# Expert weights in single blocks of 512 KB: a ring of three blocks in place of three pairs

## The chip, the cores and the metric

One core of a Trainium2 chip runs the whole program. The metric is the device time of one execution in microseconds, from runs of the same kernel on the same chip. A profile of one execution stands beside it; its times count from the start of its span.

## What is computed

Sixteen sequences x[b] of 512 rows and 512 features go through two layers.

```python
# layer 0, conditioned on one number t per sequence
h = noise_encoding(t, 128); h = silu(h @ W1 + b1); h = h @ W2 + b2
scale, shift = h @ Wsc + bsc, h @ Wsh + bsh
out = silu(scale * layernorm(x) + shift) @ W_in + b_in      # norm over rows and features
out = silu(scale * layernorm(out) + shift) @ W_out + b_out
x = out + x
# layer 1: one of 8 experts per sequence, 512 -> 2048 -> 512
g = gelu(x @ Wi[e] + bi[e]);  r = g @ Wo[e] + bo[e] + x
y = layernorm_row(r) * gamma[e] + beta[e]                    # norm over features
```

## The kernel before

Everything is kept transposed, features on the 128 partitions. A float32 product is made of three products of rounded parts: each operand is split into `hi` (rounded to float32r, a copy on ScalarE) and `lo` (the rest, a subtraction on VectorE), and `three` (L550) issues hi*hi, hi*lo and lo*hi.

**The loop.** The hidden width of 2048 is cut in 16 blocks of 128 (`HT`), so there are 256 steps `k`, 16 for each sequence. A tick `k` of the main loop (L699 for TensorE, L844 for ScalarE, L1199 for VectorE) issues `up(k)`, the first expert product of block k into a bank of `hid_ps` (12 matmuls), and `down(k-2)`, the second product of block k-2 into the four banks of `out_acc` (12 matmuls). Layer 0 of the next sequence is spread over the same ticks by the table `STAGE_AT` (L73): in ticks 2 to 5 one tile each of W_IN, in 11 to 14 one tile each of W_OUT (12 matmuls each). Below, the tick is counted within a sequence, 0 to 15. For the norm of x: `stats` in tick 13 (X_STATS, -3), `mv_out` (X_OUT) and `mv_back` (X_BACK) in tick 14, which send the statistics to DRAM and back to every partition, `totals` and `centre` in tick 15, `affine` and `silu` in tick 0, the split into `h_hi` and `h_lo` in tick 1, the first W_IN tile in tick 2. For the inner norm, `mv_back` is in tick 6 and `totals` in tick 7. The second sequence has its own table `STAGE_AT_1`.

**The splits of the weights.** In tick k ScalarE issues `gelu(k-1)`, `wi_hi_part(k+1)` (L744) and `wo_hi_part(k)` (L752); VectorE issues the lo part of gelu, `wi_lo_part(k+1)` and `wo_lo_part(k)` (L1048), which counts up the semaphore `s_wolo`. These are the readers of the weights' landing place `stage`. In the last ticks (`LAST` is 6) the downs are put off to the end, so that four ups follow each other.

**The queue.** All large loads and stores are issued by SyncE (SP), in order: a wait in its program holds up everything behind it. `expert_w` in DRAM holds the blocks in pairs, two blocks of 512 KB (half of it Wi, half Wo) side by side. `load_pair(p)` (L403) fetches a pair of 1024 KB into slot p % 3 of `stage`; the three slots take 24 KB of each partition. Pairs 0 to 2 wait for the head to be done with the slot, later ones for `s_wolo` of pair p-3. Between the pairs SP issues the other transfers: `load_x(b+2)` behind the fifth pair of a sequence, `store_y(b-2)` and `load_rows(b-1)` (gamma and beta, broadcast) behind its first pair, `load_bi(b+1)` at its end. The ACT queue carries only the small transfers of the statistics.

**The head.** Before the loop, the conditioning network runs from weights that are parked in places used later for other things: W2 in slot 0 of `stage`, the four parts of the conditioning weights `cond_raw(m)` in slots 1 and 2 (L242 to L245), a row of ones in `rows`. `s_mm2` counts that the W2 products are done, `s_mmcond` counts the four conditioning products. `w_raw[1]`, the place of W_out, is `x2_turned`, which later holds the transposed sequence.

Of the kernel before, what the change touches and what calls it, by code (L numbers as in the profile page):

```python
# [33 lines left out]
P = 128  # L34
# [7 lines left out]
B, S, D = 16, 512, 512  # L42
EMB = 128
EXPERTS, HID = 8, 2048
# [110 lines left out]
def build(nc, xT, itok, head, W1, W2, cond_w, bias_rows, affine0, affine, W_in, W_out,  # L155
          expert_w, expert_bi, expert_rows, mv_dram, y):
    ctx = ExitStack()
    with ctx:
        def sb(name, shape, dt=F32):
            return ctx.enter_context(nc.sbuf_tensor(name, shape, dt))  # L160
# [15 lines left out]
        x2_hi = [sb(f"x2_hi{n}", [P, DC, S], F32R) for n in range(2)]  # L176
        x2_lo = [sb(f"x2_lo{n}", [P, DC, S], F32R) for n in range(2)]
        NSTAGE = 3
        stage = sb("stage", [P, NSTAGE, 2, 2, 512])
        NWI, NWO = 2, 3  # L180
        wi_hi = sb("wi_hi", [P, NWI, DC, P], F32R)
        wi_lo = sb("wi_lo", [P, NWI, DC, P], F32R)
# [56 lines left out]
        w1_raw = g_sb[:, 0, :]  # L239
        t_sb, cc, small_sb = head_sb[:, 0:B], head_sb[:, B:B + 3], head_sb[:, B + 3:]  # L240
        b_in = small_sb[:, BIN:BIN + DC]
        w2_raw = stage[:, 0].rearrange("p a b n -> p (a b) n")  # L242

        def cond_raw(m):
            return stage[:, 1 + m // 2, m % 2].rearrange("p h (c n) -> p (h c) n", n=2 * P)  # L245


        b2_row, bcond_row = (x_sb[1][0:1, a:b, :].rearrange("p c n -> p (c n)") for a, b in ((0, 1), (1, 3)))
        ones = rows[0:1, 0, :]

        w_raw = [r_sb, x2_turned]

# [109 lines left out]
        @block.sync  # L362
        def _(sp):
            def load(dst, src, done):
                sp.dma_start(dst, src).then_inc(done, 16)  # L365

            def load_cond(c):
                load(cond_raw(c).rearrange("p c n -> p (c n)"), cond_w[c], ld_cond[c])

            def load_affine(c):  # L370
                load(affine_sb[:, c].rearrange("p a n -> p (a n)"), affine[c - 1], ld_affine[c])

            def load_w_in(c):
                load(w_raw[0][:, c, :], W_in[c * P:(c + 1) * P, :], ld_w_in[c])

            for c in range(DC):
                load(x_sb[0][:, c, :], xT[0, c * P:(c + 1) * P, :], ld_first[c])
                if c == 0:
                    load(w1_raw, W1, ld_w1)
            for h in range(2):  # L380
                load(half(w2_raw, h), W2[h], ld_w2[h])
            load(affine_sb[:, 0, 0, :], affine0[0], ld_affine0[0])
            for h in range(2):
                load(half(cond_raw(0), h), cond_w[0, :, h * DC * P:(h + 1) * DC * P], ld_cond0[h])
            load_w_in(0)
            load(affine_sb[:, 0, 1, :], affine0[1], ld_affine0[1])
            for c in range(1, DC):
                load_affine(c)
                load_cond(c)
                load_w_in(c)  # L390
                if c == 1:
                    load(idx[:, :], itok.rearrange("(a b) -> a b", a=1), ld_idx)
            load(w_raw[1][:, :, :].rearrange("p c n -> p (c n)"), W_out, ld_w_out)
            sp.wait_ge(ld_idx, 16)

            def load_x(b):
                if b >= 2:
                    sp.wait_ge(s_turn, len(QUADS) * (b - 1))
                else:
                    sp.wait_ge(s_blk, DC)  # L400
                load(x_sb[b % 2][:, :, :], xT[b].rearrange("(c p) n -> p c n", p=P), ld_x[b % 2])

            def load_pair(p, expert):  # L403
                slot = p % NSTAGE
                if p < NSTAGE:
                    if p:
                        sp.wait_ge(s_mmcond, 2 * p)
                    else:
                        sp.wait_ge(s_mm2, 1)
                else:  # L410
                    sp.wait_ge(s_wolo, 2 * (p - NSTAGE) + 2)
                src = expert_w[bass.ds(expert, 1), p % (HT // 2)].rearrange("e p n -> p (e n)")
                sp.dma_start(stage[:, slot].rearrange("p a b n -> p (a b n)"), src) \
                  .then_inc(ld_stage[slot], 16)

            def load_bi(b, expert):
                if b >= 2:
                    sp.wait_ge(s_ghi, HT * (b - 1))
                    sp.wait_ge(s_bo, DC * (b - 1))
                sp.dma_start(bi_sb[:, b % 2, :], expert_bi[bass.ds(expert, 1)]  # L420
                             .rearrange("e p n -> p (e n)")).then_inc(ld_bi[b % 2], 16)

            def load_rows(b, expert):
                if b >= 1:
                    sp.wait_ge(s_rout, ST * b)
                sp.dma_start(rows[:, :, :].rearrange("p a n -> p (a n)"),
                             expert_rows[bass.ds(expert, 1), :].to_broadcast([P, 2 * D])) \
                  .then_inc(ld_rows, 16)

            def store_y(b):  # L430
                sp.wait_ge(s_rout, ST * (b + 1))
                sp.dma_start(y[b].rearrange("(s p) n -> p s n", p=P), r_sb[:, :, :]) \
                  .then_inc(st_y, 16)

            expert = sp.value_load(idx[0:1, 0:1], min_val=0, max_val=EXPERTS - 1)
            per = HT // 2
            load_bi(0, expert)
            for b in range(B):
                for j in range(per):
                    load_pair(per * b + j, expert)  # L440
                    if b == 0 and j in (1, 7):
                        load_x(1 + j // 7)
                    if j == 0 and b >= 1:
                        if b >= 2:
                            store_y(b - 2)
                        load_rows(b - 1, row_expert)
                    if j == 4 and 1 <= b and b + 2 < B:
                        load_x(b + 2)
                row_expert = expert
                if b + 1 < B:  # L450
                    expert = sp.value_load(idx[0:1, b + 1:b + 2], min_val=0, max_val=EXPERTS - 1)
                    load_bi(b + 1, expert)
            store_y(B - 2)
            load_rows(B - 1, row_expert)
            for s in range(ST - 1):
                sp.wait_ge(s_rout, ST * (B - 1) + s + 1)
                sp.dma_start(y[B - 1, s * P:(s + 1) * P, :], r_sb[:, s, :]).then_inc(st_y, 16)
            for n, cols in enumerate(HALVES):
                sp.wait_ge(s_rhalf, n + 1)
                sp.dma_start(y[B - 1, (ST - 1) * P:, cols], r_sb[:, ST - 1, cols]).then_inc(st_y, 16)  # L460
            sp.wait_ge(st_y, 16 * (B - 2 + ST + len(HALVES)))
# [259 lines left out]
        def _(act):  # L721
            def copy(out, in_):
                return act.activation(out, in_, ACT.Copy)  # L723
# [18 lines left out]
                copy(w_hi[n][:, c, cols], w_raw[n][:, c, cols]).then_inc(s_whi, 1)  # L742

            def wi_hi_part(k):  # L744
                slot = k // 2 % NSTAGE
                act.wait_ge(ld_stage[slot], 16 * (k // 2 // NSTAGE + 1))
                if k >= NWI:
                    act.wait_ge(s_up, k - NWI + 1)
                copy(wi_hi[:, k % NWI].rearrange("p c n -> p (c n)"), stage[:, slot, k % 2, 0, :]) \
                    .then_inc(s_wihi, 1)  # L750

            def wo_hi_part(k):  # L752
                slot = k // 2 % NSTAGE
                if NWO <= k < EXTRA:
                    act.wait_ge(s_down, k - NWO + 1)
                copy(wo_hi_of(k), stage[:, slot, k % 2, 1, :]).then_inc(s_wohi, 1)

            def gelu(k):
                b, i = divmod(k, HT)
# [130 lines left out]
        def _(dve):  # L890
# [151 lines left out]
            def wi_lo_part(k):  # L1042
                dve.wait_ge(s_wihi, k + 1)
                lo_part(wi_lo[:, k % NWI].rearrange("p c n -> p (c n)"),
                        stage[:, k // 2 % NSTAGE, k % 2, 0, :],
                        wi_hi[:, k % NWI].rearrange("p c n -> p (c n)")).then_inc(s_wilo, 1)

            def wo_lo_part(k):  # L1048
                dve.wait_ge(s_wohi, k + 1)
                lo_part(wo_lo_of(k), stage[:, k // 2 % NSTAGE, k % 2, 1, :], wo_hi_of(k)) \  # L1050
                    .then_inc(s_wolo, 1)

            def r_evac(b, s):
# [205 lines left out]
        def _(pool):  # L1259
# [35 lines left out]
            pool.memset(x2_hi[0][:, 0, :].bitcast(F32), 0.0).then_inc(s_zero, 1)  # L1295
            pool.memset(enc_sin[:, B:], 0.0).then_inc(s_pad, 1)
            pool.memset(m1[:, :, B:], 0.0).then_inc(s_pad, 1)
            pool.memset(ones, 1.0).then_inc(s_ones, 1)
            pool.wait_ge(s_half, 1)
            first_rstd(0)  # L1300
            for c in range(1, DC - 1):
# [2 lines left out]
                                   ALU.subtract).then_inc(s_wlopool, 1)  # L1304
            first_rstd(1)
            norm_rstd(1, 0)
            pool.memset(eye_raw[:, :], 1.0).then_inc(s_ones, 1)
            pool.wait_ge(s_ones, 2)
            pool.affine_select(out=eye_raw[:, :], in_=eye_raw[:, :], pattern=[[-1, P]], base=0,
                               channel_multiplier=1, compare_op=ALU.is_equal, fill=0.0).then_inc(s_eye, 1)  # L1310
            for k in ticks:
# [11 lines left out]
def pack_experts(Wi, Wo):  # L1323


    wi = Wi.reshape(EXPERTS, DC, P, HT, P).transpose(0, 3, 2, 1, 4).reshape(EXPERTS, HT, P, D)
    wo = Wo.reshape(EXPERTS, HT, P, D)
    both = np.concatenate([wi, wo], axis=3).reshape(EXPERTS, HT // 2, 2, P, 2 * D)
    return np.ascontiguousarray(both.transpose(0, 1, 3, 2, 4).reshape(EXPERTS, HT // 2, P, 4 * D))


# [44 lines left out]
```

## Time and profile before

| | |
|---|---|
| time of the runs, median (lowest to highest of 3) | 1772.29 us (1772.17 to 1772.65) |
| span of the profiled execution | 1771.7 us |
| TensorE busy | 1762.8 us, 99% |
| VectorE, ScalarE, GpSimd busy | 1286.2 us (73%), 977.2 us (55%), 69.0 us (4%) |
| DMA | 189.35 MB, mean 107 GB/s |
| mean granted TensorE clock | 0.999 |

The profiled execution has no total time of its own beside the span; the median of the runs is 0.6 us above it. The page is read in this way: first the busy shares and the chain that ended last, which name the engine that sets the time; then what this engine waited for; then the timelines of the other engines, which show how early each of its inputs is ready.

### The profile page before, as it was taken

To read this page: it belongs to the slowest core of one execution; us is meant where nothing else is said; L and a number is where in the kernel's file an instruction comes from. 1 tells how busy PE (TensorE), PEld (TensorE's weight loads), DVE (VectorE), ACT (ScalarE), POOL (GpSimd) and SP (SyncE) were. 2 spreads that over 40 slices of the span, in tenths; PEclk is the share of its full clock that TensorE was granted. 3 is DMA by queue.
4 is the path that set the end of the run, shared out by engine and by line. 5 is a ranking of instruction groups with operands and counts; after the bars stand their busy time and mean duration, and the time that the engine had idled before them with its cause. 6 is when DMAs were issued, how large, how long until landed. Compare 5 with 4: busy or idle time off the path is not lost.

```text
span 1771.7 us, 22300 instructions
## 1 busy us (share of the span) xinstructions
PE 1762.8 (99%) x7939; PEld 1454.3 (82%) x7939; DVE 1286.2 (73%) x2147; ACT 977.2 (55%) x1551; POOL 69.0 (4%) x138
## 2 busy tenths in 40 slices
PE   9999999999999999999999999999999999999998
PEld 6888888888888888888888888888888888888887
DVE  6876777767677777767777677677777777777576
ACT  4756554565545656456564555645556555565442
POOL 1100000000000000000000000000000000000000
PEclk9999999999999999999999999999999999999999
DMA  7332232322333233232332313333133232422321
GB/s 292 99 111 75 99 111 85 143 76 99 110 120 111 75 123 110 99 110 72 122 110 99 113 69 122 112 121 110 53 139 113 98 110 75 143 87 75 114 104 68
DMA packets 51666, 189.35 MB, mean 107 GB/s; under 512 B 10467, under 2 KB 14563, under 8 KB 35044
## 3 DMA queue, kind: packets, MB, share of 16 engines
q1 hardware_dynamic: 42770, 183.94, 29.3%
q10 hardware_dynamic: 8786, 3.99, 1.8%
q8 instruction: 64, 1.05, 0.3%
q14 instruction: 46, 0.38, 0.1%
HBM read 171.10 MB, written 16.81 MB: 106 GB/s over the span
## 4 chain that ended last, share of the span: by engine, by line
PE 99%; DMA 1%; SPq 0%; DVE 0%; issue 0%; ACT 0%; POOL 0%; DVEq 0%
PE out_acc L553 39%; PE hid_ps L553 39%; PE blk_ps L553 18%; DMA stage<-in_cond_w 1%; SPq L365 0%; PE out_acc L583 0%; PE out_acc L594 0%; PE out_acc L595 0%; PE out_acc L598 0%; PE hid_ps L571 0%; PE blk_ps L571 0%; PE out_acc L571 0%; PE hid_ps L598 0%; PE hid_ps L594 0%; PE blk_ps L594 0%; PE hid_ps L595 0%
## 5 line engine op out<-in xcount | busy, mean ns | idle before, releaser
L553 PE MATMUL hid_ps<-x_hi,wi_lo 128*128 128x512 f32 x1020 | 396.8, 389 | 0.0
L553 PE MATMUL hid_ps<-x_lo,wi_hi 128*128 128x512 f32 x1020 | 396.8, 389 | 0.0
L553 PE MATMUL hid_ps<-x_hi,wi_hi 128*128 128x512 f32 x1020 | 396.8, 389 | 0.0
L553 PE MATMUL out_acc<-wo_hi,g_hi 128*128 128x512 f32 x1012 | 393.7, 389 | 0.0
L553 PE MATMUL out_acc<-wo_lo,g_hi 128*128 128x512 f32 x1012 | 393.7, 389 | 0.0
L553 PE MATMUL out_acc<-wo_hi,g_lo 128*128 128x512 f32 x1012 | 393.7, 389 | 0.0
L765 ACT ACTIVATE g_sb<-hid_ps,bi_sb 128x512 f32<-128x512 f32 x256 | 175.9, 687 | 311.3 <-PE hid_ps L553 311.0
L893 DVE TENSOR_TENSOR g_lo<-g_sb,g_hi 128x512 fp32r<-128x512 f32 x253 | 173.1, 684 | 190.9 <-ACT g_hi L769 189.2
L723 ACT ACTIVATE wo_hi<-stage 128x512 fp32r<-128x512 f32 x253 | 160.1, 633 | 172.1 <-PE out_acc L553 172.1
L553 PEld LDWEIGHTS hid_ps<-x_hi,wi_lo 128*128 128x128 f32 x1020 | 191.6, 188 | 39.8
L553 PEld LDWEIGHTS hid_ps<-x_hi,wi_hi 128*128 128x128 f32 x1020 | 191.6, 188 | 39.7
L553 PEld LDWEIGHTS hid_ps<-x_lo,wi_hi 128*128 128x128 f32 x1020 | 191.4, 188 | 39.6
L893 DVE TENSOR_TENSOR wo_lo<-stage,wo_hi 128x512 fp32r<-128x512 f32 x253 | 174.3, 689 | 67.0 <-ACT wo_hi L723 63.3
L553 PEld LDWEIGHTS out_acc<-wo_lo,g_hi 128*128 128x128 f32 x1012 | 190.1, 188 | 39.4
L553 PEld LDWEIGHTS out_acc<-wo_hi,g_hi 128*128 128x128 f32 x1012 | 189.9, 188 | 39.5
L553 PEld LDWEIGHTS out_acc<-wo_hi,g_lo 128*128 128x128 f32 x1012 | 189.9, 188 | 39.2
L553 PE MATMUL blk_ps<-h_hi,w_hi 128*128 128x512 f32 x480 | 186.7, 389 | 0.0
L553 PE MATMUL blk_ps<-h_lo,w_hi 128*128 128x512 f32 x480 | 186.7, 389 | 0.0
L553 PE MATMUL blk_ps<-h_hi,w_lo 128*128 128x512 f32 x480 | 186.7, 389 | 0.0
L1036 DVE STREAM_TRANSPOSE x_turned<-x 32x512 f32<-32x512 f32 x256 | 179.6, 702 | 7.5
L893 DVE TENSOR_TENSOR wi_lo<-stage,wi_hi 128x512 fp32r<-128x512 f32 x256 | 174.8, 683 | 0.5 <-ACT wi_hi L723 0.5
L769 ACT ACTIVATE g_hi<-hid_ps,bi_sb 128x512 fp32r<-128x512 f32 x253 | 172.5, 682 | 0.0
(172 smaller groups left out, 1647.9 us busy)
## 6 DMA issues: line engine op xcount, KB each, us to landing
stage<-in_expert_w SPq DMA_DIRECT2D x128, 1024.0 KB, 4.8
x<-in_xT SPq DMA_DIRECT2D x15, 1024.0 KB, 7.4
out_y<-r_sb SPq DMA_DIRECT2D x15, 1024.0 KB, 5.1
rows<-in_expert_rows SPq DMA_DIRECT2D x16, 512.0 KB, 6.7
mv_all<-mv_dram ACTq DMA_DIRECT2D x30, 128.0 KB, 3.8
affine_sb<-in_affine SPq DMA_DIRECT2D x3, 512.0 KB, 10.0
stage<-in_cond_w SPq DMA_DIRECT2D x3, 512.0 KB, 10.9
x<-in_xT SPq DMA_DIRECT2D x4, 256.0 KB, 4.5
```

The lines of the kernel that those rows point to most:

```text
L553: last = pe.matmul(dst, w[wp], xs[xp], start=start and i == 0, stop=stop and i == 2)
L723: return act.activation(out, in_, ACT.Copy)
L765: act.activation(g_sb[:, k % 2, :], hid_ps[k % 2][:, :], ACT.Gelu, bias=bi_sb[:, b % 2, i:i + 1]).then_inc(s_gelu, 1)
L769: act.activation(g_hi_of(k), hid_ps[k % 2][:, :], ACT.Gelu, bias=bi_sb[:, b % 2, i:i + 1]).then_inc(s_ghi, 1)
L893: return dve.tensor_tensor(out, full, hi.bitcast(F32), ALU.subtract)
L1036: dve.transpose(dst[:, :, :, h, :], src[:, :, :, s, :]).then_inc(s_turn, 1)
```

## The change

`stage` has three slots of one block (512 KB; 12 KB of each partition in all) instead of three slots of a pair (24 KB). Each block is loaded by itself as soon as its slot is free, so 256 loads of 512 KB take the place of 128 loads of 1024 KB, and `pack_experts` keeps the blocks apart. At most three blocks are in `stage` in place of six. The other transfers of SP stand at corresponding places between the blocks: `load_x(b+2)` behind the tenth block, store and rows behind the second. As `stage` no longer holds the weights of the head, W2 goes to `x2_turned`, and the load of W_out into the same place gets a wait for `s_mm2`; the conditioning weights go to the three slots and to `rows`; the ones lie in the buffer of the identity matrix, which is made from them with a wait for the conditioning products.

```diff
-        stage = sb("stage", [P, NSTAGE, 2, 2, 512])
+        stage = sb("stage", [P, NSTAGE, 2, 512])
...
-        w2_raw = stage[:, 0].rearrange("p a b n -> p (a b) n")
+        w2_raw = x2_turned
 
         def cond_raw(m):
-            return stage[:, 1 + m // 2, m % 2].rearrange("p h (c n) -> p (h c) n", n=2 * P)
+            at = stage[:, m] if m < NSTAGE else rows
+            return at[:, :, :].rearrange("p h (c n) -> p (h c) n", n=2 * P)
...
-        ones = rows[0:1, 0, :]
+        ones = eye_raw[0:1, 0:BLOCK]
...
+            sp.wait_ge(s_mm2, 1)
             load(w_raw[1][:, :, :].rearrange("p c n -> p (c n)"), W_out, ld_w_out)
...
-            def load_pair(p, expert):
-                slot = p % NSTAGE
-                if p < NSTAGE:
-                    if p:
-                        sp.wait_ge(s_mmcond, 2 * p)
-                    else:
-                        sp.wait_ge(s_mm2, 1)
+            def load_block(k, expert):
+                slot = k % NSTAGE
+                if k < NSTAGE:
+                    sp.wait_ge(s_mmcond, k + 1)
                 else:
-                    sp.wait_ge(s_wolo, 2 * (p - NSTAGE) + 2)
-                src = expert_w[bass.ds(expert, 1), p % (HT // 2)].rearrange("e p n -> p (e n)")
-                sp.dma_start(stage[:, slot].rearrange("p a b n -> p (a b n)"), src) \
-                  .then_inc(ld_stage[slot], 16)
+                    sp.wait_ge(s_wolo, k - NSTAGE + 1)
+                src = expert_w[bass.ds(expert, 1), k % HT].rearrange("e p n -> p (e n)")
+                sp.dma_start(stage[:, slot].rearrange("p a n -> p (a n)"), src).then_inc(ld_stage[slot], 16)
...
             for b in range(B):
-                for j in range(per):
-                    load_pair(per * b + j, expert)
-                    if b == 0 and j in (1, 7):
-                        load_x(1 + j // 7)
-                    if j == 0 and b >= 1:
+                for j in range(HT):
+                    load_block(HT * b + j, expert)
+                    if b == 0 and j in (2, 15):
+                        load_x(1 + j // 15)
+                    if j == 1 and b >= 1:
                         if b >= 2:
                             store_y(b - 2)
                         load_rows(b - 1, row_expert)
-                    if j == 4 and 1 <= b and b + 2 < B:
+                    if j == 9 and 1 <= b and b + 2 < B:
                         load_x(b + 2)
...
             def wi_hi_part(k):
-                slot = k // 2 % NSTAGE
-                act.wait_ge(ld_stage[slot], 16 * (k // 2 // NSTAGE + 1))
+                slot = k % NSTAGE
+                act.wait_ge(ld_stage[slot], 16 * (k // NSTAGE + 1))
...
-            pool.memset(ones, 1.0).then_inc(s_ones, 1)
+            pool.memset(eye_raw[:, :], 1.0).then_inc(s_ones, 1)
...
-            pool.memset(eye_raw[:, :], 1.0).then_inc(s_ones, 1)
-            pool.wait_ge(s_ones, 2)
+            pool.wait_ge(s_ones, 1)
+            pool.wait_ge(s_mmcond, DC)
```

The other readers of `stage` change their index in the same way, and `pack_experts` returns the blocks unpaired.

## Rows read from the trace of the kernel before

**Rows 1.** Page: busy time with share and instructions; chain that ended last.

```profile
PE 1762.8 (99%) x7939; PEld 1454.3 (82%) x7939; DVE 1286.2 (73%) x2147; ACT 977.2 (55%) x1551; POOL 69.0 (4%) x138
...
PE 99%; DMA 1%; SPq 0%; DVE 0%; issue 0%; ACT 0%; POOL 0%; DVEq 0%
```

**Rows 2.** Windows: stretch, length, busy us and instructions per engine, clock, DMA share, GB/s.

```profile
706.30:815.10 108.80, 108.80 (x482) 90.12 (x481) 79.69 (x133) 60.85 (x97) 3.77 (x8) 1.00 0.32 105
```

**Rows 3.** Waits of TensorE: who waited for whom, us in total, times, longest.

```profile
PE hid_ps L471 <- DMA stage<-in_cond_w: 1.7, 1, 1.7
PE hid_ps L480 <- POOL x_hi L1295: 1.4, 1, 1.4
```

**Rows 4.** Page, DMA issues: count, KB each, median us from issue to landing.

```profile
stage<-in_expert_w SPq DMA_DIRECT2D x128, 1024.0 KB, 4.8
x<-in_xT SPq DMA_DIRECT2D x15, 1024.0 KB, 7.4
...
out_y<-r_sb SPq DMA_DIRECT2D x3, 256.0 KB, 2.0
```

**Rows 5.** Line L413 (loads of expert pairs), all 128: time to landing.

```profile
DMA to landing us min/median/max: 4.6/4.8/13.6
```

**Rows 6.** Timeline of ACT and DVE, ticks 6 to 9 of a batch: start, length.

```profile
739.33 0.68 DVE L893 TENSOR_TENSOR wo_lo<-stage,wo_hi 128x512 fp32r<-128x512 f32 x1
744.23 0.69 DVE L893 TENSOR_TENSOR wo_lo<-stage,wo_hi 128x512 fp32r<-128x512 f32 x1 [0.38 <-ACT wo_hi L723]
...
747.44 0.63 ACT L723 ACTIVATE wi_hi<-stage 128x512 fp32r<-128x512 f32 x1
...
752.88 0.63 ACT L723 ACTIVATE wi_hi<-stage 128x512 fp32r<-128x512 f32 x1
```

**Rows 7.** Timeline of DVE and ACT, ticks 2 to 4 of the first batch.

```profile
57.56 0.68 DVE L893 TENSOR_TENSOR wo_lo<-stage,wo_hi 128x512 fp32r<-128x512 f32 x1
...
66.63 0.68 DVE L893 TENSOR_TENSOR wi_lo<-stage,wi_hi 128x512 fp32r<-128x512 f32 x1
...
62.00 0.63 ACT L723 ACTIVATE wi_hi<-stage 128x512 fp32r<-128x512 f32 x1
```

**Rows 8.** Timeline of DVE, ACT and PE in the last ticks.

```profile
1739.75 0.69 DVE L893 TENSOR_TENSOR wo_lo<-stage,wo_hi 128x512 fp32r<-128x512 f32 x1 [0.81 <-ACT wo_hi L723]
...
1744.58 0.63 ACT L723 ACTIVATE wi_hi<-stage 128x512 fp32r<-128x512 f32 x1 [0.41 <-PE hid_ps L553]
...
1747.05 0.39 PE L553 MATMUL hid_ps<-x_hi,wi_hi 128*128 128x512 f32 x1
```

**Rows 9.** Timeline from tick 14 to the first W_IN tile of the next batch.

```profile
790.47 0.69 DVE L893 TENSOR_TENSOR wo_lo<-stage,wo_hi 128x512 fp32r<-128x512 f32 x1
799.24 0.29 DVE L927 BATCH_NORM_STATS2 mean_bn<-mv_all 128x6 f32<-128x128 f32 x1
...
804.07 0.69 DVE L893 TENSOR_TENSOR wo_lo<-stage,wo_hi 128x512 fp32r<-128x512 f32 x1 [0.30 <-ACT wo_hi L723]
...
812.83 2.49 DVE L893 TENSOR_TENSOR h_lo<-work,h_hi 128x512 fp32r<-128x512 f32 x4
...
793.32 0.33 ACTq L822 DMA_DIRECT2D mv_all<-mv_dram  x1
...
814.09 0.39 PE L553 MATMUL blk_ps<-h_hi,w_hi 128*128 128x512 f32 x1
```

**Rows 10.** Tile `mv_all`, all 30 loads: time to landing.

```profile
DMA to landing us min/median/max: 2.9/3.8/6.5
```

**Rows 11.** DMA issues of the window 730 to 760 us, with the load of tick 6.

```profile
mv_all<-mv_dram ACTq DMA_DIRECT2D x1, 128.0 KB, 5.3
```

**Rows 12.** Timeline of the head: second half of the W2 products; issue of W_out's load.

```profile
10.77 0.65 PE L471 MATMUL out_acc<-stage,m 128*32 128x128 f32 x16
...
12.22 0.43 SPq L365 DMA_DIRECT2D x_turned<-in_W_out  x1
```

More of the change, by code:

```diff
@@ L435, in _ @@
             expert = sp.value_load(idx[0:1, 0:1], min_val=0, max_val=EXPERTS - 1)
-            per = HT // 2
             load_bi(0, expert)
             for b in range(B):
-                for j in range(per):
-                    load_pair(per * b + j, expert)
-                    if b == 0 and j in (1, 7):
-                        load_x(1 + j // 7)
-                    if j == 0 and b >= 1:
+                for j in range(HT):
[3 more added lines that the diff above has]
+                    if j == 1 and b >= 1:
                         if b >= 2:
@@ L744, in wi_hi_part @@
             def wi_hi_part(k):
-                slot = k // 2 % NSTAGE
-                act.wait_ge(ld_stage[slot], 16 * (k // 2 // NSTAGE + 1))
+                slot = k % NSTAGE
+                act.wait_ge(ld_stage[slot], 16 * (k // NSTAGE + 1))
                 if k >= NWI:
                     act.wait_ge(s_up, k - NWI + 1)
-                copy(wi_hi[:, k % NWI].rearrange("p c n -> p (c n)"), stage[:, slot, k % 2, 0, :]) \
+                copy(wi_hi[:, k % NWI].rearrange("p c n -> p (c n)"), stage[:, slot, 0, :]) \
                     .then_inc(s_wihi, 1)
             def wo_hi_part(k):
-                slot = k // 2 % NSTAGE
+                slot = k % NSTAGE
                 if NWO <= k < EXTRA:
                     act.wait_ge(s_down, k - NWO + 1)
-                copy(wo_hi_of(k), stage[:, slot, k % 2, 1, :]).then_inc(s_wohi, 1)
+                copy(wo_hi_of(k), stage[:, slot, 1, :]).then_inc(s_wohi, 1)
             def gelu(k):
@@ L1044, in wi_lo_part @@
                 lo_part(wi_lo[:, k % NWI].rearrange("p c n -> p (c n)"),
-                        stage[:, k // 2 % NSTAGE, k % 2, 0, :],
+                        stage[:, k % NSTAGE, 0, :],
                         wi_hi[:, k % NWI].rearrange("p c n -> p (c n)")).then_inc(s_wilo, 1)
@@ L1049, in wo_lo_part @@
                 dve.wait_ge(s_wohi, k + 1)
-                lo_part(wo_lo_of(k), stage[:, k // 2 % NSTAGE, k % 2, 1, :], wo_hi_of(k)) \
+                lo_part(wo_lo_of(k), stage[:, k % NSTAGE, 1, :], wo_hi_of(k)) \
                     .then_inc(s_wolo, 1)
@@ L1327, in pack_experts @@
     wo = Wo.reshape(EXPERTS, HT, P, D)
-    both = np.concatenate([wi, wo], axis=3).reshape(EXPERTS, HT // 2, 2, P, 2 * D)
-    return np.ascontiguousarray(both.transpose(0, 1, 3, 2, 4).reshape(EXPERTS, HT // 2, P, 4 * D))
+    return np.ascontiguousarray(np.concatenate([wi, wo], axis=3))
 def kernel(**inputs):
```

## The prediction

> **What bounds the kernel now.** I read the page first. TensorE is busy for 1762.8 us of a span of 1771.7 us, and the chain that ended last is 99% TensorE [rows 1]. One whole batch in the middle (window 706.3 to 815.1) has TensorE busy for all of its 108.80 us, at full granted clock [rows 2]. The waits of TensorE come to a few microseconds, all in the head: 1.7 us for the conditioning weights, 1.4 us for the first memset [rows 3]. So nothing outside TensorE costs time unless a matmul stands still for it. The change adds and removes no matmul. I therefore ask of each moved transfer how long it may now take, and whether TensorE feels it if it takes longer.
>
> **The ring in the steady state.** In before, pair p is fetched when `wo_lo` of the second block of pair p-3 is done. After, block k is fetched when `wo_lo` of block k-3 is done, and ScalarE's `wi_hi` of block k is the first reader. Call tick k the turn of the loop in which `up(k)` runs; `wi_hi(k)` runs in tick k-1. The window of block k is thus from the end of `wo_lo(k-3)` to the start of `wi_hi(k)`, some 1 1/2 to 2 ticks. I placed all 16 windows of the batch in the DVE and ACT timelines. The narrowest is block 9: `wo_lo(6)` ends at 739.33 + 0.69 = 740.02, `wi_hi(9)` starts at 747.44 [rows 6], 7.4 us. The others have 8.0 to 13.4 us.
>
> What does 512 KB cost? The trace of before has no such weight load. From above: a whole pair of 1024 KB lands in 4.8 us at the median, 4.6 us at least [rows 4, 5]. From below: a 256 KB store on the same queue lands in 2.0 us [rows 4]. The straight line between these (2.8 us for 768 KB) gives 2.0 + 2.8/3 = 2.9 us. The load is nearer to its own kind, so I take 3.4 us, an estimate, and 4.6 us as the upper end. Add 0.3 us, my allowance for SP to wake up. 3.7 (or 4.9) us against 7.4 us: no wait.
>
> The queue is in order, so what stands ahead of a block counts. The x load of 1024 KB now goes out behind block 9 (before, behind the pair of blocks 8 and 9). It is issued at about 740.8 and takes 7.4 us [rows 4], so it ends near 748.2. Block 10, issued when `wo_lo(7)` ends (744.23 + 0.69 = 744.9), can be ready by 748.2 + 3.4 = 751.6, and its reader starts at 752.88 [rows 6]. Margin 1.3 us, and with the upper end about 0. Even then TensorE has more: `up(10)` comes in the next tick. Cost nothing; the cover is the tick between split and matmul, and if it were gone each late microsecond would be paid once a batch.
>
> A sentence on a rule against this change. The Trainium skill (DMA: Bandwidth & Descriptors, section Measured under Bandwidth) advises transfers of 1 MiB and more to reach three quarters of peak; this change halves them. Its fit (section Anatomy of one DMA) of 2.0 us plus bytes over 436 GB/s, given for another issuing path, makes 3.2 us of 512 KB, an estimate from that page; by it the sum stays the same.
>
> Costs of issue: 128 more loads on SP, each a third of a microsecond. SP only issues and waits; it waits for `wo_lo` throughout and computes nothing, so this is hidden. Nor do new waits hold others up: the store of y and the load of rows wait for `r_out` of tick 12 and are now reached in tick 14; the x load waits for the transposes of tick 5 and is reached in tick 6.
>
> **The first batch.** Blocks 0 to 2 go out in the head, well before use. The narrowest window of the kernel is block 5: `wo_lo(2)` ends at 57.56 + 0.68 = 58.24, `wi_hi(5)` starts at 62.00 [rows 7], 3.8 us against my 3.7 (up to 4.9). ScalarE may start `wi_hi(5)` late by up to 1.1 us. But VectorE reads that result only at 66.63 [rows 7], 4.6 us after 62.00. Cost nothing. The x load of batch 2 now goes out behind block 15, two or three ticks later than before, and may land about when VectorE first reads it, in tick 13. I bound its lateness at 2 us; the statistics that read it feed TensorE only five ticks later, so it costs nothing.
>
> **The tail.** The last four ups follow each other without downs, so ticks shrink. Block 255 waits for `wo_lo(252)`, which ends at 1739.75 + 0.69 = 1740.44; `wi_hi(255)` starts at 1744.58 and `up(255)` at 1747.05 [rows 8]. Landing: 1740.44 + 3.7 = 1744.1 (upper 1745.3). With the upper value the two splits (0.63 and 0.69 us) end at 1746.7, still before 1747.05. Cost nothing, 0.4 us to spare at worst.
>
> **The head.** W_out's load now waits for the W2 products, since W2 lies where W_out goes. These products end at 10.77 + 0.65 = 11.42, and SP reaches the load at 12.22 anyway [rows 12]. The wait is met on arrival. Queued behind it on SP are the expert loads; they move by nothing. Block 0 waits for the first conditioning products, block 1 for the second, block 2 for the third; half the bytes of the first pair stand ahead of block 1. The ones row moves into the eye buffer: the memset is a 128x128 one in place of a 1x512 one, the second memset is gone, and the new wait before the select is for products of the head, long done. Cost and gain nothing. The wait of 1.7 us in the head [rows 3] is for a load issued before anything that moves.
>
> **The one transfer that now has company.** From the third batch on, SP issues one block, the store of y (1024 KB) and the load of rows (512 KB) back to back, once a batch. Before, they went out in tick 12. After, they are reached when `wo_lo` of tick 14 ends, 790.47 + 0.69 = 791.2 [rows 9], so their 2 MB run from about 791 to 800. Into this falls `mv_back` of the x norm, issued on the ACT queue at 793.32; VectorE uses it at 799.24 [rows 9], 5.9 us later. Before, the 30 loads of this kind landed in 3.8 us at the median and 6.5 us at most [rows 10]. The one at 738.13, which shares the engines with an x load, took 5.3 us [rows 11]; the others of tick 6 that I looked up lie in this upper part of the spread, those of tick 14 in the lower. So I expect 5.3 to 6.5 us here, 13 times (the norms of batches 3 to 15).
>
> How late may it be? From the totals at 799.24 the chain is centre, affine, silu, h_hi, h_lo, then the first W_IN tile. VectorE has 0.30 us idle ahead of `wo_lo` at 804.07. The first h_lo ends at 812.83 + 0.69 = 813.52 and the tile starts at 814.09: 0.57 us more [rows 9]. Together 0.87 us: a landing up to 5.9 + 0.87 us, less 0.1 us that I allow for the semaphore, so 6.7 us after issue, costs TensorE nothing. The worst seen, 6.5 us, is inside. I take zero, with 0.2 us between the bound and the cliff. In return tick 6 is relieved of the x load, where there was no stall to give back.
>
> **Sum.** 1771.7 us of the profiled span plus nothing. The median of the runs is 1772.29 us, 0.6 us above that span (what lies around it), so the forecast is 1772.3 us.
>
> **The rivals.**
> A, slower by the stall of `mv_back`: store and rows together hold the short load up longer than the x load does. It decides from a landing of 6.7 us. At 7.7 us (another 1.2 us above the worst seen) each of 13 batches loses 1.0 us: 1772.3 + 13 = 1785 us. Above 0.2%, 3.5 us, it comes from an average of 7.0 us. For it: two large transfers in place of one. Against: the slow ones so far stay within 6.5 us [rows 10]. Chance of over 3.5 us: 6%; of less, 5%.
> By the Trainium skill (DMA: Bandwidth & Descriptors, section Queues, rings and completion order) an engine takes turns between queues a packet of several descriptors at a time, so one short transfer waits for about one foreign packet whatever the backlog. By that rule it would stay at the lengths seen beside the x load, and the sum would be my forecast; the trace agrees so far, with 5.3 us beside an x load of 1024 KB [rows 11].
> B, the ring is too short: a 512 KB load takes far more than half a pair, because waits between loads expose the fixed part. The tail feels it first, from a landing of about 5.0 us; at 6.6 us it loses 1.6 us once, 1774 us. In every batch it would need over 7 us. Chance 5% for the small case, 2% for more than 3.5 us.
> C, faster: the head's first reader of the ring gets its block sooner and the tick 6 load is alone. All waits of TensorE in these rows are 3.1 us [rows 3], so even losing every one gives 1769 us, inside 0.2%. Chance beyond that 2%.
> D, the ring doesn't change the pace at all because each load is still tied to `wo_lo`. That is the forecast itself: fetches come as late as before or later, and no reader waits.
>
> **Numbers.** Forecast 80%; A 11%, B 7%, C 2%. A measurement tells about 0.2%, 3.5 us. Slower by more: 6 + 2 = 8%. Faster 2%. Within: 90%. The range takes the small cases of A and B: 1771.0 to 1775.0 us.
>
> **What would show it.** Right: no wait of TensorE for `wi_lo`, `h_lo` or stage outside the head; 256 weight loads landing near 3.4 us; `mv_all` landing later at tick 14 and earlier at tick 6; TensorE busy for all of a batch of 108.8 us. Wrong: batches longer than 108.8 us with TensorE idle ahead of the first W_IN tile (A), or waits of ScalarE for stage that reach TensorE (B).

## The result, and the profile after

The kernel after takes 1786.49 us at the median (1783.76 to 1789.04, 4 runs), the kernel before, run with it, 1772.23 us (1771.62 to 1772.65, 4 runs). The ratio is 1.008, interval 1.0068 to 1.0092: slower by 14 us. The forecast was 1772.3 us, with a range of 1771.0 to 1775.0. Rival A, the stall of `mv_back`, had been priced at 1785 us.

Three lines of the page of after: busy time, then the chain that ended last. They answer to [rows 1].

```profile
span 1785.0 us, 22684 instructions
...
PE 1767.2 (99%) x7939; PEld 1454.1 (81%) x7939; DVE 1286.3 (72%) x2147; ACT 976.5 (55%) x1551; POOL 66.1 (4%) x137
...
PE 86%; DMA 5%; DVE 5%; ACT 2%; issue 2%; SPq 0%; DVEq 0%; ACTq 0%; POOL 0%
```

TensorE still looks "99% busy", so the table of busy shares would hide the loss. The chain does not: 14% of it now runs over other engines and DMA, against 1% in [rows 1]. The waits say where. Waits of after: who waited for whom, us in total, times, longest.

```profile
PE blk_ps L550 <- DVE h_lo L890: 10.4, 11, 2.6
PE hid_ps L477 <- POOL x_hi L1292: 1.4, 1, 1.4
PE blk_ps L468 <- DMA stage<-in_cond_w: 0.2, 1, 0.2
DVE mean_bn L924 <- DMA mv_all<-mv_dram: 21.3, 14, 3.5
ACT wi_hi L720 <- DMA stage<-in_expert_w: 0.9, 1, 0.9
```

The first row is new: [rows 3] have no such wait. VectorE waits for the 128 KB load `mv_all`, and 11 times that reaches the first W_IN tile. The spans differ by 1785.0 - 1771.7 = 13.3 us. They split so: 10.4 us of waits for `h_lo`, 1767.2 - 1762.8 = 4.4 us more busy time of TensorE (taken apart below), and 1.5 us less wait for the conditioning weights in the head (1.7 us in [rows 3], 0.2 us here). 10.4 + 4.4 - 1.5 = 13.3 us. The 1.5 us are no gain of the change. The first expert product begins at 46.97 us in before and at 45.34 us in after; in e1, e2 and e3 below, which have the head of after, it begins at 46.66, 45.70 and 45.36 us, and in e4, with the head of before, at 46.05 us.

One batch from the inside. Timeline of after, one slice: start, length, engine, line, and in brackets idle time and who ended it. `mv_dram` is the 1 KB write of the statistics to DRAM, `mv_all` the load of them back to every partition.

```profile
901.77 0.33 ACTq L812 DMA_DIRECT2D mv_dram<-mv  x1
...
903.87 0.33 SPq L412 DMA_DIRECT2D stage<-in_expert_w  x1
904.25 0.43 SPq L430 DMA_DIRECT2D out_y<-r_sb  x1
904.87 0.36 SPq L424 DMA_DIRECT2D rows<-in_expert_rows  x1
906.71 0.33 ACTq L819 DMA_DIRECT2D mv_all<-mv_dram  x1
...
915.37 0.29 DVE L924 BATCH_NORM_STATS2 mean_bn<-mv_all 128x6 f32<-128x128 f32 x1 [3.50 <-DMA mv_all<-mv_dram]
...
929.40 0.47 PE L550 MATMUL blk_ps<-h_hi,w_hi 128*128 128x512 f32 x1 [2.61 <-DVE h_lo L890]
```

SP issues block, y and rows within 1.4 us; 1.8 us behind the rows (1.0 us in most batches) the small load goes out on the ACT queue. The DMA issues of the window from 903.8 to 907 us (KB, us to landing) show when each arrives:

```profile
out_y<-r_sb SPq DMA_DIRECT2D x1, 1024.0 KB, 7.9
stage<-in_expert_w SPq DMA_DIRECT2D x1, 512.0 KB, 4.9
rows<-in_expert_rows SPq DMA_DIRECT2D x1, 512.0 KB, 10.8
mv_all<-mv_dram ACTq DMA_DIRECT2D x1, 128.0 KB, 8.6
```

The rows land at 904.87 + 10.8 = 915.7 us, the small load at 906.71 + 8.6 = 915.3 us: together with the last of the 2 MB issued ahead of it. In the 13 batches it lands after 7.3, 7.5, 7.5, 6.3, 8.4, 7.0, 8.6, 7.4, 7.6, 8.0, 6.4, 7.4 and 7.0 us. The two batches with 6.3 and 6.4 us lose nothing.

The packets of the load, too, begin late. Queue q1 carries SP's transfers and q10 those of ACT. DMA of the first 3.6 us behind the issue of the small load, in after (906.71 to 910.3 us): packets, MB, share of the 16 engines.

```profile
q1 hardware_dynamic: 574, 1.39, 100.6%
```

Not one packet of q10 is among them. In the 13 batches of after the first one starts 3.5 to 4.1 us behind the issue; in tick 14 of before, with nothing ahead, 1.0 to 1.1 us. From there on packets of both queues run side by side, and until the load lands it takes another 2.4 to 4.9 us.

Windows of after: length, then busy us and instructions of PE, PEld, DVE, ACT and POOL, granted clock, DMA share, GB/s; the third is the batch that follows the landing of 6.3 us, the last a slice behind the stall of 2.61 us (which ended at 929.40).

```profile
466.90:576.60 109.70, 109.05 (x482) 90.00 (x481) 79.69 (x132) 60.79 (x96) 3.42 (x8) 1.00 0.34 104
906.70:1019.90 113.20, 110.59 (x481) 91.11 (x480) 79.62 (x133) 60.80 (x96) 3.76 (x8) 0.98 0.34 101
576.60:685.40 108.80, 108.80 (x482) 90.09 (x481) 79.70 (x132) 60.82 (x96) 3.76 (x8) 1.00 0.32 105
931.00:932.00 1.00, 1.00 (x4) 0.80 (x3) 1.00 (x3) 1.00 (x2) 0.00 (x0) 0.50 0.42 168
```

The batch of 906.7 to 1019.9 us is 4.4 us longer than one without loss ([rows 2]): 2.6 us idle and 1.8 us more busy. That second part is mostly clock. Behind the stall the granted clock stood at 0.50, the 1.2 GHz level, and the chain shows 12 matmuls of one shape at two speeds:

```profile
929.40 4.57 PE blk_ps L550 x12
...
936.71 2.72 PE out_acc L550 x12
```

So twelve matmuls took 4.57 us where they take 2.72 us at full clock: 1.85 us on top of a stall of 2.6 us. But this is the only stretch of the loop of after in which the clock fell. The first window shows what the other ten stalls add at a granted clock of 1.00: 109.05 us busy in place of 108.80, 0.25 us beyond the wait itself. In the timeline matmuls of a steady stream start every 0.227 us, and each is recorded with 0.389 us; the last one before a gap is charged in full (0.16 us), and the first one behind it starts its successor after 0.31 us (0.08 us). The 4.4 us more busy time are thus 1.8 us behind the one fall of the clock and some 2.6 us at full clock.

### The profile page after: what moved, and what is told of

Same layout as the page of the kernel before. It is cut to its first block, busy times and chain, and to the rows that moved or that the text cites. A ratio compares the mean times of both kernels' runs of the same rounds, so it can differ in the third digit from the quotient of the medians.

```text
span 1785.0 us, 22684 instructions
## 1 busy us (share of the span) xinstructions
PE 1767.2 (99%) x7939; PEld 1454.1 (81%) x7939; DVE 1286.3 (72%) x2147; ACT 976.5 (55%) x1551; POOL 66.1 (4%) x137
## 4 chain that ended last, share of the span: by engine, by line
PE 86%; DMA 5%; DVE 5%; ACT 2%; issue 2%; SPq 0%; DVEq 0%; ACTq 0%; POOL 0%
PE hid_ps L550 33%; PE out_acc L550 33%; PE blk_ps L550 18%; DMA mv_all<-mv_dram 4%; ACT work L779 1%; DVE work L966 1%; DVE wi_lo L890 1%; DVE wo_lo L890 1%; ACT L762 1%; DMA stage<-in_cond_w 1%; DMA mv_dram<-mv 1%; DVE g_lo L890 0%; SPq L366 0%; ACT g_hi L766 0%; DVE x L1011 0%
## 5 line engine op out<-in xcount | busy, mean ns | idle before, releaser
L550 PE MATMUL blk_ps<-h_hi,w_hi 128*128 128x512 f32 x480 | 188.2, 392 | 10.4 <-DVE h_lo L890 10.4
```

Of the source, the lines that this page charges most:

```text
L550: last = pe.matmul(dst, w[wp], xs[xp], start=start and i == 0, stop=stop and i == 2)
```

## Experiments

Two theories at first. T: the two large transfers together ahead of the small load. R: the ring itself, with its blocks of half the size and twice the number of loads. Then, within T: T1, what counts is the bytes issued ahead; T2, what runs beside the load counts, whatever the order. Lines below are edits of the kernel after unless said otherwise; the median of before, run beside them, stands with each time.

**e1, both transfers one tick earlier; the ring as in after**

```
-                    if j == 1 and b >= 1:
+                    if j == 0 and b >= 1:
```

> The changed kernel with one thing different: the store of y and the load of rows go out behind the first block of a batch instead of the second, one tick earlier (tick 13 in place of 14), the ring of single blocks kept. Theory T (the store and the rows collide with the statistics' way through DRAM in tick 14): the loads of mv_all at tick 14 land in 3 to 4 us again, TensorE waits for no h_lo, time 1770.5 to 1772.5 us. Theory R (the thinner ring or its 256 loads cost the time by themselves): 1785 to 1787 us, as the changed kernel.

1772.92 us against 1772.17 (ratio 1.0002, 0.9992 to 1.0011). Tile `mv_all` of e1, all 30 loads; no wait of TensorE for `h_lo` is left:

```profile
DMA to landing us min/median/max: 2.9/3.5/5.4
```

The whole loss is gone with the ring of single blocks unchanged (the median lies 0.4 us above the range of T). R falls. The earlier place is not free of effect, though. In 12 of 13 batches the 1 KB write `mv_dram` landed after 5.0 to 5.8 us in place of 2.5 to 3.8 us in tick 14 of before, so that the small load went out 0.9 to 1.7 us late; it then landed in 3.2 to 4.5 us, which keeps the sum below what TensorE can bear.

**e2 and e3, only one of the two in tick 14**

e2 (y in tick 14, rows in tick 13):

```
+                    if j == 0 and b >= 1:
+                        load_rows(b - 1, row_expert)
+                    if j == 1 and b >= 2:
+                        store_y(b - 2)
```

> The changed kernel, with only the load of rows moved one tick earlier; the store of y stays behind the second block. Theory T, shared by size: with 1.5 MB (one block and the store) ahead in place of 2 MB, mv_all at tick 14 lands in 5.5 to 6.7 us, time 1771 to 1776 us. If the store is the whole cause: landing 7 us and more, 1783 to 1787 us. Theory R: 1785 to 1787 us.

e3 (rows in tick 14, y in tick 13) has the two swapped.

> The changed kernel, with only the store of y moved one tick earlier; the load of rows stays behind the second block. Theory T, shared by size: 1 MB ahead, mostly gone when the small load starts, landing 4 to 5.5 us, time 1770.5 to 1772.5 us. If rows (many partitions reading one line of DRAM) is the cause: landing 7 us and more, 1783 to 1787 us. Theory R: 1785 to 1787 us.

e2: 1772.56 us (1.0002, 0.9992 to 1.0012); e3: 1772.10 us (0.9999, 0.999 to 1.0009). With block and y ahead (1.5 MB) the load of tick 14 lands after 5.4 to 6.1 us (4.1 us once), with block and rows (1 MB) after 3.7 to 6.6 us, up to 1.1 us above what was expected. Tile `mv_all` of e2, then of e3, all 30 loads:

```profile
DMA to landing us min/median/max: 3.1/3.9/6.1
```

```profile
DMA to landing us min/median/max: 2.9/3.7/6.6
```

Both stay inside 6.7 us and neither loses anything. Neither transfer does it alone; it takes both. In e2 the first packet is just as late as in after (3.3 to 4.4 us behind the issue, but for that one batch), and from there the load takes another 1.2 to 2.5 us, against 2.4 to 4.9 us in after: the rows lengthen this second part.

**e4, before with its pairs, both transfers as late as in after**

```
                         if b >= 2:
+                            sp.wait_ge(s_wolo, HT * b - 1)
                             store_y(b - 2)
```

> The kernel before, ring of three pairs, with one wait added on SP: the store of y and the load of rows are held until wo_lo of tick 14 is done, the moment at which the changed kernel issues them. Theory T: the loads of mv_all at tick 14 land in 6.5 to 8.5 us and TensorE waits for h_lo, time 1780 to 1787 us. Theory R: the pairs are unharmed, 1772 to 1773 us.

1807.22 us (1.0205, 1.0188 to 1.0222): the ring of before is slowed by the placement too, more than after is. Here a pair of 1 MB stands in the row, 2.5 MB in all, and the load lands after 8.8 us at the median (5.6 to 9.6). Page and waits of e4, and a window behind one stall:

```profile
PE 1773.9 (98%) x7939; PEld 1458.5 (81%) x7939; DVE 1286.5 (71%) x2147; ACT 977.0 (54%) x1551; POOL 69.0 (4%) x138
...
PE blk_ps L554 <- DVE h_lo L894: 22.3, 12, 2.8
...
716.50:718.00 1.50, 1.50 (x5) 1.20 (x4) 1.50 (x4) 0.54 (x1) 0.00 (x0) 0.50 0.19 77
```

22.3 us of waits and 1773.9 - 1762.8 = 11.1 us more busy time of TensorE make 33 us; five stretches at 0.50 lie in that busy time. I had expected 1780 to 1787 us: direction right, size wrong, since I had counted neither the pair nor the clock.

**e6, other bytes of the same amount in their place.** This kernel does additional loads which no one reads; y and rows go out in tick 13 as in e1.

```
+                    if j == 1 and b >= 2:
+                        sp.wait_ge(ld_spare, 32 * (b - 2))
+                        load(spare[:, 0:DC, :], xT[b].rearrange("(c p) n -> p c n", p=P), ld_spare)
+                        load(spare[:, DC:DC + 2, :].rearrange("p a n -> p (a n)"), affine[0], ld_spare)
```

> The changed kernel with the store of y and the load of rows one tick earlier, and in their old place two loads that nothing uses, of the same sizes: 1024 KB of x and 512 KB of affine weights into a spare buffer. It does more work than the reference asks: 14 times 1.5 MB of loads. If bytes ahead are what counts, whatever their direction: mv_all at tick 14 lands in 6.5 to 8 us, time 1779 to 1787 us. If writes to DRAM or the broadcast of rows are what counts: landing 4 to 6.5 us, 1771.5 to 1774 us.

1789.83 us against 1772.54 (1.0099, 1.008 to 1.0117). So it is neither the direction of the store nor what the rows are. The time is 2.8 us above the range expected. The landings were shorter than in after, 6.0 to 7.7 us, but the small load was issued 3.1 us behind the block instead of 2.0, since the 1 KB write of the statistics, on which it waits, was late as well (4.9 to 5.8 us in 12 of 13 batches, as in e1, where y and rows also go out in tick 13). The row of waits:

```profile
PE blk_ps L557 <- DVE h_lo L897: 12.8, 12, 2.4
```

**e7, both transfers one tick later**

```
-                    if j == 1 and b >= 1:
+                    if j == 2 and b >= 1:
```

> The changed kernel with the store of y and the load of rows behind the third block of a batch, one tick later (tick 15). The load of mv_all is over by then. Theory T: landing 3 to 4.5 us, no wait of TensorE, 1771.5 to 1773 us. If it were lateness of y or rows that cost the time (a reader of rows, or r_sb not yet free), it would get worse: over 1787 us.

1772.32 us (0.9999, 0.999 to 1.0009). Landings of tick 14 are 3.3 to 4.8 us, and a batch is full again. Window of e7, columns as above:

```profile
684.20:793.00 108.80, 108.80 (x482) 90.09 (x481) 79.71 (x132) 60.80 (x97) 3.76 (x8) 1.00 0.33 105
```

One tick before or one tick behind costs nothing; only tick 14 does.

**e5 and e8, holding the transfers back.** e5 holds y (and with it the rows) until the write of the statistics has landed; e8 has the same wait between y and rows.

```
                             if b + 1 < B:
                                 sp.wait_ge(st_mv, 16 * (2 * b + 1))
```

> The changed kernel with one wait added on SP: the store of y and the load of rows are held until the norm's statistics have landed in DRAM, so that they start at the same time as the load of mv_all or up to 1 us earlier, in place of 2 us earlier. Theory T1 (what delays the small load is what already stands in SP's queue ahead of it): mv_all at tick 14 lands in 5 to 6.5 us, as in tick 6 of the kernel before, where 2 MB were queued at the same moment; time 1771.5 to 1776 us. Theory T2 (any overlap with 1.5 MB of store and rows costs the same): landing 7 to 8 us, time 1780 to 1787 us.

> The changed kernel with only the load of rows held until the statistics have landed in DRAM; the store of y goes out as in the changed kernel. Theory T1: the rows stand behind the small load or beside its start, mv_all lands as with the store alone, 5.5 to 6.3 us, time 1771.5 to 1774 us. Theory T2: the same bytes overlap, landing 7 us and more, 1780 to 1787 us.

e5: 1781.50 us against 1772.54 (1.0057, 1.004 to 1.0073). e8: 1789.31 us against 1772.54 (1.0099, 1.0079 to 1.012). The time of e5 lies in the range of T2, that of e8 above both ranges. But neither made the order that it was meant to make. ScalarE comes to `mv_back` only a microsecond or more after the wait is met, so in e5 y was mostly still 1.1 to 1.6 us ahead, and in e8 the rows 0.6 to 1.0 us. By time both are inconclusive. But e5 holds a comparison within itself: a batch in which the two went out at the same instant, against one of the usual ones. Timeline of e5, then the landing of the small load, for either:

```profile
357.34 0.40 SPq L430 DMA_DIRECT2D out_y<-r_sb  x1
357.35 0.38 ACTq L821 DMA_DIRECT2D mv_all<-mv_dram  x1
...
mv_all<-mv_dram ACTq DMA_DIRECT2D x1, 128.0 KB, 4.5
```

```profile
464.77 0.40 SPq L430 DMA_DIRECT2D out_y<-r_sb  x1
...
466.05 0.33 ACTq L821 DMA_DIRECT2D mv_all<-mv_dram  x1
...
mv_all<-mv_dram ACTq DMA_DIRECT2D x1, 128.0 KB, 8.2
```

4.5 us beside y, 8.2 us with y 1.3 us ahead. There is one more batch of the first kind, with 5.4 us; the other eleven have 6.3 to 8.8 us. That speaks for T1, and e9 was made to put it to the test.

e8 holds a comparison too, and it speaks against the sharp form of T1. In two of its batches the rows went out 0.14 us behind the small load, with block and y (1.5 MB) ahead as in e2, and yet it landed after 7.4 and 9.2 us, where e2 has 5.4 to 6.1. Timeline and issues of the first:

```profile
358.13 0.33 ACTq L821 DMA_DIRECT2D mv_all<-mv_dram  x1
358.27 0.33 SPq L424 DMA_DIRECT2D rows<-in_expert_rows  x1
...
rows<-in_expert_rows SPq DMA_DIRECT2D x1, 512.0 KB, 7.5
mv_all<-mv_dram ACTq DMA_DIRECT2D x1, 128.0 KB, 7.4
```

The first packet comes 4.2 us behind the issue in both. I read it so, without a further run: behind such a late start, what is issued just after the load still runs beside it and lengthens it.

**e9, both transfers in the same tick, but behind the small load**

```
                         if b >= 2:
+                            sp.wait_ge(s_x2hi, DC * b + DC)
                             store_y(b - 2)
```

> The changed kernel, with the store of y and the load of rows held on SP until ScalarE's last x2_hi of tick 14 is done, which puts their issue about 0.7 us behind the issue of the load of mv_all, in place of 2 us ahead. The transfers still overlap in time. Theory T1 (what stands in SP's queue ahead of the small load delays it): landing 4 to 5.5 us in all 13 batches, no wait of TensorE for h_lo, time 1771.5 to 1774 us. Theory T2 (overlap as such): landing 7 us and more, 1780 to 1787 us.

1772.54 us against 1772.77 (0.9999, 0.9989 to 1.0009); no wait for `h_lo`. Timeline of e9, the landing of that load, and the tile's 30 loads:

```profile
466.10 0.33 ACTq L820 DMA_DIRECT2D mv_all<-mv_dram  x1
466.76 0.40 SPq L430 DMA_DIRECT2D out_y<-r_sb  x1
...
mv_all<-mv_dram ACTq DMA_DIRECT2D x1, 128.0 KB, 4.3
```

```profile
DMA to landing us min/median/max: 2.9/3.4/6.0
```

The same bytes run beside the load, but behind it: 4.3 us in this batch, 3.4 to 5.8 us in the 12 batches of this order, instead of 7.4 at the mean. The 6.0 us belong to the one batch where y was 0.14 us ahead. The DMA of e9 in the same 3.6 us behind the issue (466.10 to 469.69 us):

```profile
q1 hardware_dynamic: 321, 0.89, 61.8%
q10 hardware_dynamic: 138, 0.13, 11.5%
```

138 of the load's 144 packets are under way, where after has none; the first starts 1.3 to 2.0 us behind the issue. As the whole cause T2 falls: what was issued before the load decides when its packets begin. What runs beside it lengthens the rest, as e2 and e8 show.

**e10, before with `mv_back` of tick 6 moved behind the x load and its pair (one run)**

The edit takes `mv_back(b, 1)` out of tick 6 and puts it behind `gelu` of tick 7.

> The kernel before, with the load of mv_all of the inner norm moved from tick 6 to the start of tick 7, behind that tick's gelu: about 3 us behind the x load and the pair, in place of beside them. The same 2 MB, the same transfers, only the small load comes later into them. Theory T1: its landing grows from 5.2 to 6.5 us to 6.5 to 8.5 us. Theory T2: it stays at 5.2 to 6.5 us or falls, as part of the overlap is gone. The time is not the question here; it may rise in both, as the totals are due at once.

1774.84 us against 1772.77. The landings mostly missed the 6.5 to 8.5 us that T1 expected, at 5.4 to 5.6 us, with four of 6.4 to 6.7 us; by the number, T2 was right. The rows of one of those say why. DMA issues of e10 and their landings:

```profile
740.01 0.37 SPq L413 DMA_DIRECT2D stage<-in_expert_w  x1
...
stage<-in_expert_w SPq DMA_DIRECT2D x1, 1024.0 KB, 8.7
...
742.19 0.33 ACTq L822 DMA_DIRECT2D mv_all<-mv_dram  x1
...
mv_all<-mv_dram ACTq DMA_DIRECT2D x1, 128.0 KB, 6.7
```

The pair lands at 748.7 us and the small load at 748.9. It lands with the backlog; issued 2.2 us behind it, it is charged only for what is left. As a test of T1's number it failed; that the load lands with the rest of the backlog is a reading made afterwards, which the rows agree with. The 2 us of time are mostly one stall of 1.6 us, at 124 us, before the steady state.

**Together.** Landing of the load of tick 14, by what SP had issued up to some 2 us before: 0.5 MB 3.3 to 4.8 us (e7), 1 MB 3.7 to 6.6 us (e3), 1.5 MB 5.4 to 6.1 us (e2, one of 4.1), 2 MB 7.4 us on average (after), 2.5 MB 8.8 us (e4, median). In tick 6 of e10 2 MB issued 2.2 to 2.8 us ahead give 5.4 to 6.7 us, so bytes alone do not set it. TensorE stands still from 6.9 us on (below). The first packet follows the same order: 1.3 to 2.1 us behind the issue with the block alone ahead (e7, e9), 2.6 to 4.0 us with the rows too (e3), 3.3 to 4.4 us with y (e2, but for one batch), 3.5 to 4.1 us with both (after).

What stays open: why the first packet of the ACT queue starts later the more SP has issued before, and what holds the 1 KB write up. A transfer that SP took 3 us to issue (y once in e2, the rows once in after) went with a shorter landing (4.1 and 6.3 us), for which I have no row that shows the cause. A mended placement has no gain over before: e1, e2, e3, e7 and e9 all lie within 0.1% of it.

## Why the prediction was wrong, step by step

**The failed step: "So I expect 5.3 to 6.5 us here".** The bound came from tick 6, where one x load of 1 MB is issued at the same moment as the small load, 738.11 us against 738.13 us, with nothing much queued before it; it landed after 5.3 us [rows 11]. In tick 14 it is 2 MB, issued some 1 to 2 us ahead. My nearest row was near by kind but not by order, and by e9 order is what decides most of it. The landing was 7.4 us at the mean, 0.9 us above my upper end, and I had called a landing between 6.5 and 6.7 us safe on 0.2 us of margin. The text had the data to be more careful: its own sentence puts the 2 MB "from about 791 to 800", and a load that ends with them, issued at 793.3, lands after 6.7 us, right at the cliff.

The rule that the prediction set beside it leaned the wrong way. As I read the Trainium skill (DMA: Bandwidth & Descriptors, section Queues, rings and completion order), an engine takes turns between queues a packet at a time. That a short load therefore waits for about one foreign packet "whatever the backlog" was my inference; the section does not say it. The traces disagree with it: with 0.5 MB ahead the load lands in 3.3 to 4.8 us, with 2 MB in 7.4 us, and e9 brings it down by order alone. Once packets of both queues are under way they do run side by side, but in after the first one of the ACT queue starts only 3.5 to 4.1 us behind the issue. The measurement decides.

**The cliff was right to 0.2 us.** It lies at 6.9 us behind the usual issue: 6.3 and 6.4 us cost nothing, 7.05 us costs 0.19 us, and in the batch shown 8.64 us of landing and 0.84 us of late issue less the wait of 2.61 us leave 6.87 us; the other stalls give the same. The prediction's 6.7 us was 5.9 + 0.87 us less its allowance of 0.1 us, so it erred on the safe side, and the failure is in the landing alone.

**Rival A's mechanism was right and its chance wrong.** It had 1.0 us in each of 13 batches; it became 0.8 us of waiting in the mean over the 13 (two have none) and 0.3 us more busy time. That its 1785 us comes so near to the measured 1786.49 us is partly luck: its example of 7.7 us was 0.3 us above the mean landing, and two terms were missing from it. In 3 of 13 batches `mv_back` itself went out 0.7 to 0.8 us late, since the 1 KB write `mv_dram` ahead of it landed after 4.8 to 4.9 us instead of 2.8 to 3.9. And each stall brings 0.25 us more busy time, the longest one 1.8 us, since the clock fell behind it.

**The ring: right.** Page of after, and line L412 (all 256 loads):

```profile
stage<-in_expert_w SPq DMA_DIRECT2D x256, 512.0 KB, 3.2
```

```profile
DMA to landing us min/median/max: 3.0/3.2/10.7
```

3.2 us at the median against the 3.4 us estimated; ScalarE waits for them once, in the first batch, and never in the steady state. Rival B falls.

**First batch: right.** `wi_hi(5)` waited 0.9 us, forecast up to 1.1, and TensorE did not feel it, nor the 1.0 to 1.9 us of the same wait in the other runs with this ring. **Tail: right**, no DMA wait there: `wi_hi(255)` waited for none. **Head: right**; W_out's wait was met on arrival (the W2 products end at 11.39 us, the load goes out at 11.86 us), and the difference there is scatter, as shown above. **Relief in tick 6: right**, the loads land after 3.2 to 4.1 us, and it gives nothing back. **Rival C:** nothing.

**The frame: slightly off.** I put 0.6 us around the span of the profiled run. In the profiled run of after it is 1786.85 - 1785.0 = 1.8 us; the runs of before beside the experiments have spans of 1770.0 to 1771.8 us, so the profiled one, with 1771.7 us, was among the longest. The two slips cancel, which is luck, and harmless here.

## What to carry to other kernels

A small transfer that a computation waits for can land as late as the large ones issued ahead of it, even from another queue; so when large transfers are moved in time, look which short round trip is issued in the two microseconds behind their new place, and add up the bytes ahead of it. A bound taken from the nearest row must match in order of issue as well as in kind and size. A slack of 0.2 us on a path that repeats in every batch is a coin to be tossed, not cover, and a stall can cost more than its wait: 0.25 us more at full clock here, and 1.8 us where the clock fell.

## What the runs showed of the hardware

- Order of issue between two queues: 128 KB on the ACT queue landed after 3.4 to 5.8 us with the 1.5 MB of y and rows issued on SP's queue from 0.5 to 0.7 us behind it (e9), and after 7.4 us at the mean with the same bytes 0.7 to 2.5 us ahead (after). The first packet started 1.3 to 2.0 us behind the issue in e9, and 3.5 to 4.1 us in after.
- A 1 KB write to DRAM took 2.5 to 3.9 us to land in tick 14 of before and in ten of 13 batches of after, 4.8 to 4.9 us in three batches of after, and 5.0 to 5.8 us in 12 of 13 batches of e1, with y and rows issued 5 to 6 us ahead of it; so both legs of a round trip by way of DRAM can be slowed.
- The granted clock fell from full (2.4 GHz) to 0.50 (1.2 GHz) behind a stall of 2.6 us in after; one W_IN tile took 4.57 us in place of 2.72. It did not fall behind the ten shorter stalls (up to 1.5 us), and not behind one of 2.4 us in e6 either.
- A weight load of 512 KB lands in 3.2 us and one of 1024 KB in 4.8 us, and for this kernel the smaller size is no handicap: e1, with single blocks, ran at 1.0002 of before, with 12 KB less of SBUF in each partition.
